# First scan step summed on TensorE, image 0's copy ahead of its shift: a four-layer residual stack on one core

## What is computed

```python
def _L0_conv_ref(x, w1, b1, w2, b2, w3, b3, alpha):     # layer 2 is the same
    xf = x.reshape(n, c, hw)
    e1 = jax.nn.relu(jnp.einsum('dc,ncp->ndp', w1, xf) + b1[None, :, None])
    e2 = jax.nn.relu(jnp.einsum('dc,ncp->ndp', w2, xf) + b2[None, :, None])
    assembly = jax.nn.relu(jnp.einsum('oc,ncp->nop', w3, xf) + b3[None, :, None])
    attn = jax.nn.softmax(jnp.einsum('ndi,ndj->nij', e1, e2), axis=-1)
    out = jnp.einsum('ncj,nij->nci', xf, attn)
    return (alpha[0] * out + assembly).reshape(n, c, h, w)

def step(prev, x_i):                                     # layer 1; layer 3 has relu for the slope
    y = jnp.einsum('oc,nch->noh', Wc, prev) + conv_b[None, :, None]
    y = jnp.where(y >= 0, y, prelu_a * y)
    cur = y + x_i
    return (cur, cur)

x = x + layer_l(_gn(x))                                  # for l = 0, 1, 2, 3
```

## Time and profile before

| | us |
|---|---|
| median of the three runs | 257.13 (256.96 to 257.18) |
| the profiled execution | 256.91 |
| its span, first to last instruction | 255.1 |
| TensorE busy (products / weight loads) | 245.5 / 218.1 |
| VectorE busy | 171.8 |
| ScalarE busy | 95.6 |
| GpSimd busy | 86.6 |

### The profile page before, as it was taken

One profiled execution on the slowest core, in us unless ns is written; L12 is line 12 of the kernel. 1 busy time (PEld: TensorE's weight loads), 2 busy tenths in 40 slices (PEclk: granted clock), 3 DMA queues, 4 the chain that ended last, 5 costly groups with the idle time before them and its releaser, 6 DMA issues.

```text
span 255.1 us, 11065 instructions
## 1 busy us (share of the span) xinstructions
PE 245.5 (96%) x4485; PEld 218.1 (85%) x4488; DVE 171.8 (67%) x667; ACT 95.6 (37%) x229; POOL 86.6 (34%) x135
## 2 busy tenths in 40 slices
PE   6997999999978999999999999999999999999995
PEld 2776888888668999999997787878786999999995
DVE  2779857475767777777789785666758555555453
ACT  2144463724963343434445445454557100000000
POOL 0206600004346656666732310000062433243332
PEclk9999999999999999999999999999999999999999
DMA  6999000000000000000000000000000000011212
GB/s 219 393 374 421 37 0 0 4 0 0 0 4 3 0 0 0 1 0 0 0 1 3 0 0 4 0 0 0 1 3 0 3 0 0 0 41 62 82 62 82
DMA packets 5199, 11.47 MB, mean 45 GB/s; under 512 B 704, under 2 KB 3264, under 8 KB 4672
## 3 DMA queue, kind: packets, MB, share of 16 engines
q1 hardware_dynamic: 4896, 10.76, 11.4%
q10 hardware_dynamic: 288, 0.52, 0.6%
HBM read 9.19 MB, written 2.10 MB: 44 GB/s over the span
## 4 chain that ended last, share of the span: by engine, by line
PE 88%; DVE 6%; DMA 2%; POOL 2%; issue 1%; ACT 0%; POOLq 0%; DVEq 0%; ACTq 0%
PE banks L494 43%; PE banks L391 20%; PE banks L456 11%; PE banks L403 6%; PE banks L422 2%; DMA x<-in_x 2%; PE banks L334 1%; PE banks L441 1%; PE banks L477 1%; DVE st L682 1%; POOL rstd L1065 1%; DVE mx L792 1%; PE banks L358 1%; DVE sloped L923 0%; PE banks L369 0%
## 5 line engine op out<-in xcount | busy, mean ns | idle before, releaser
L494 PE MATMUL banks<-state,wc 128*64 128x64 f32 x3840 | 114.9, 223 | 2.7 <-DVE state L933 1.3
L494 PEld LDWEIGHTS banks<-state,wc 128*64 128x64 f32 x3840 | 114.1, 138 | 3.7 <-DVE state L933 1.6
L391 PE MATMUL banks<-xn,w 128*128 128x256 f32 x256 | 61.0, 384 | 0.0
L391 PEld LDWEIGHTS banks<-xn,w 128*128 128x128 f32 x256 | 47.1, 190 | 7.2 <-issue 1.7
L1065 POOL TENSOR_TENSOR rstd<-gvar,mhalf 128x2 f32<-128x2 f32 (+1 forms) x12 | 15.2, 1279 | 104.2 <-DVE gvar L757 100.2
L906 DVE SCALAR_TENSOR_TENSOR state<-banks,negb,inb 128x64 f32<-128x64 f32 x116 | 29.1, 281 | 24.1 <-PE banks L494 24.0
L923 DVE SCALAR_TENSOR_TENSOR sloped<-banks,par,share 128x64 f32<-128x64 f32 x116 | 29.7, 281 | 14.1 <-PE banks L494 12.0
L456 PE MATMUL banks<-probT,xT 128*128 128x256 f32 x128 | 29.0, 380 | 1.4 <-DVE probT L830 1.4
L456 PEld LDWEIGHTS banks<-probT,xT 128*128 128x128 f32 x128 | 24.3, 190 | 5.0 <-issue 1.8
L631 ACT COPY banks<-inb 128x256 f32 (+1 forms) x29 | 10.9, 376 | 31.9 <-DVE state L933 29.4
L1122 POOL TENSOR_TENSOR share<-share,bent 128x256 f32<-128x256 f32 x29 | 17.7, 612 | 4.1 <-ACT share L632 3.2
(11 more groups left out here) (113 smaller groups left out, 228.5 us busy)
## 6 DMA issues: line engine op xcount, KB each, us to landing
w<-in_w SPq DMA_DIRECT2D x2, 1024.0 KB, 12.0
xT<-in_xT SPq DMA_DIRECT2D x4, 512.0 KB, 12.3
wc<-in_wc SPq DMA_DIRECT2D x2, 1024.0 KB, 17.5
result<-xh SPq DMA_DIRECT2D x15, 128.0 KB, 1.8
x<-in_x SPq DMA_DIRECT2D x3, 512.0 KB, 8.4
x<-in_x ACTq DMA_DIRECT2D x1, 256.0 KB, 4.3
x<-in_x SPq DMA_DIRECT2D x1, 256.0 KB, 4.1
w<-in_w ACTq DMA_DIRECT2D x1, 256.0 KB, 4.8
```

The costliest lines, as they stand in the source:

```text
L391: mm = nc.tensor.matmul(bank[2 + m // 2][:, m % 2 * POS:(m % 2 + 1) * POS], w3[l][:, k, m * P:(m + 1) * P], xn_s[:, k], start=(k == 0), st ...
L494: mm = nc.tensor.matmul(bank[K * h + m][c:c + TILE, 0:COLS], wc[l][:, k, m * P + c:m * P + c + TILE], state[:, h, k], start=first and not ...
```

## The change

- *Step 0 of the first scan.* `prelu_sum` and its semaphores go. The products of step 0 leave their accumulation open, and TensorE adds the inputs by products with the identity matrix (`add_inputs`): for output columns 0 and 1 after the last product of column 2, for columns 2 and 3 at the end. VectorE then makes slope and maximum from the bank.
- *Shares of steps 0 and 1 in parts.* ScalarE makes them for the first three images ahead of the last image's inputs, and for the last image when `early` is there; of the four late input columns (L616) one instead of two goes ahead of that.
- *GpSimd in the first scan.* The biased share of step 1 goes ahead of the keeping of state 0, and the sum for the very last step (L1118) behind the keeping of states 1 and 2. The loop starts at state 3 and keeps a state before it does the next share, where it did the share first; both orders are the same sequence.
- *Image 0 of layer 0.* The copy of half 1 of `probT` goes ahead of `shifted_input` and of all four residuals.
- *The power of layer 0* is taken for image 1 alone first (four columns) and then for images 2 and 3 (eight columns), each with its own negated mean and shift; the waits on `norm[0].done` and `s_shift` count one more.
- *Layer 2's signed weights* wait for outputs of layer 0: the small ones for the first of image 0, the large ones for the first of image 1 (two columns) and of image 2 (two columns).
- *Passage into layer 2.* The means stand behind three groups of transposes, not four, the variances behind five, not six; two of image 1's four statistics go behind the normalised image.

```diff
+        def power_rounds(l):
+            rounds = [(r, c0, c1) for r, (c0, c1) in enumerate(norm_rounds(l))]
+            return rounds if l else [rounds[0], (1, K, 2 * K), (1, 2 * K, NC)]
...
+            def add_inputs(ms):
+                s = scan[1]
+                for m in ms:
+                    if m == 0:
+                        pe.wait_ge(s.inb, NC - K)
+                        pe.wait_ge(s.early, K + 1)
+                    nc.tensor.matmul(bank[m][:, 0:COLS], ident[:], inb[:, 1, m], start=False, stop=True,
+                                     skip_group_check=True).then_inc(s.y[m], 1)
...
+                alone = l == 1 and not seeded
...
-                            state[:, h, k], start=first and not seeded, stop=final, skip_group_check=True)
-                    if final:
+                            state[:, h, k], start=first and not seeded, stop=final and not alone,
+                            skip_group_check=True)
+                    if final and alone:
+                        add_inputs({2: (0, 1), 3: (2, 3)}.get(m, ()))
+                    elif final:
                         mm.then_inc(s.y[m], 1)
...
-                    turn(range(0, 4))
+                    turn(range(0, 3))
                     group_means(l, r)
-                    turn(range(4, 6))
+                    turn(range(3, 5))
                     group_variances(l, r)
-                    turn(range(6, 8))
+                    turn(range(5, 8))
...
-                        act.wait_ge(norm[l].done, 2)
+                        act.wait_ge(norm[l].done, 2 if first or l else 3)
...
-                scan_inputs(1, 1, (N - 1,), EARLY, range(K // 2))
+                ready, late = slice(0, (N - 1) * T), slice((N - 1) * T, COLS)
+                def first_share(q, places):
+                    return nc.scalar.activation(share[:, q, :, places], inb[:, q + 1, :, places], ACT.Identity,
+                                                scale=oma[:, 0:1])
                 act.wait_ge(s.inb, NC - K)
+                first_share(0, ready)
+                first_share(1, ready)
+                scan_inputs(1, 1, (N - 1,), EARLY, range(1))
                 act.wait_ge(s.early, K + 1)
-                step_inputs(0, 1, 0)
-                step_inputs(1, 2, 1)
-                scan_inputs(1, 1, (N - 1,), EARLY, range(K // 2, K))
+                first_share(0, late).then_inc(s.share, 1)
+                act.wait_ge(s.cleared, 1)
+                nc.scalar.copy(banks[:, K:2 * K, 0:COLS], inb[:, 2]).then_inc(s.seeded, 1)
+                first_share(1, late).then_inc(s.share, 1)
+                scan_inputs(1, 1, (N - 1,), EARLY, range(1, K))
...
-                        shifted_input()
+                        if l == 2:
+                            shifted_input()
...
-                    add_residual(0)
-                    add_residual(1)
+                    late = first and l == 0
+                    early = 0 if late else 2
+                    for m in range(early):
+                        add_residual(m)
                     dve.wait_ge(s.pt_mm, n * PC + 2)
                     nc.vector.tensor_copy(by_rows(l, probT[:, 1]), in_order(l, bank[0][:, 0:POS])).then_inc(s.pt_copied, 1)
-                    for m in range(2, by_vector[l] if last else K):
+                    if late:
+                        shifted_input()
+                    for m in range(early, by_vector[l] if last else K):
                         add_residual(m)
...
-                        for k in range(K):
-                            prelu_sum(q, t, h, k)
...
-                    image_stats(l, 1)
+                    image_stats(l, 1, range(K // 2))
                 normalise_first(l)
+                if l == 2:
+                    image_stats(l, 1, range(K // 2, K))
...
-                for r, (c0, c1) in enumerate(norm_rounds(l)):
-                    width = K // 2 if c1 - c0 == K else c1 - c0
+                for r, c0, c1 in power_rounds(l):
+                    width = K // 2 if c1 - c0 == K and (l, r) != (0, 1) else c1 - c0
...
+                if l == 1:
+                    share_bias(1, 1)
+                    pool.wait_ge(s.sloped[K - 1], 1)
+                nc.gpsimd.tensor_tensor(inb[:, 0], state[:, 0], bias, ALU.add).then_inc(s.taken, 1)
+                def keep_state(t, h):
+                    for u in units:
+                        pool.wait_ge(s.state[u], t + 1)
+                    nc.gpsimd.tensor_tensor(inb[:, t], state[:, h], bias, ALU.add).then_inc(s.taken, 1)
+                    if l == 1:
+                        share_bias(t + 1, 1 - h)
+                keep_state(1, 1)
+                keep_state(2, 0)
+                pool.wait_ge(s.taken, 1)
+                nc.gpsimd.tensor_tensor(by_image(inb[:, 0]), by_image(inb[:, 0]), xr[:, 0], ALU.add).then_inc(s.last_in, 1)
+                with pool.Fori(0, (T - 4) // 2) as i:
                     for h in range(2):
+                        keep_state(i * 2 + 3 + h, 1 - h)
...
+                        pool.wait_ge(att[0].x_done, 1 if done is s_signed12 else K * (1 + k // 2) + 1)
                         nc.gpsimd.tensor_tensor(w[:, k], w[:, k], sign[:, 0:1].to_broadcast([P, w.shape[2]]), ALU.mult)\
                             .then_inc(done, 1)
```

More of the change, by code:

```diff
@@ L120, in __init__ @@
             self.sloped = [sem(f"sloped_branch_ready_{u}") for u in units]
-            self.summed = [sem(f"first_products_summed_{u}") for u in units]
             self.cleared = sem("banks_cleared")
@@ L624, in step_inputs @@
                 s = scan[1]
-                if isinstance(q, int) and q == 1:
-                    act.wait_ge(s.cleared, 1)
-                elif not (isinstance(q, int) and q == 0):
-                    for k in range(K):
-                        act.wait_ge(s.state[k], q)
-                if not (isinstance(q, int) and q == 0):
-                    nc.scalar.copy(banks[:, K * h:K * h + K, 0:COLS], inb[:, t]).then_inc(s.seeded, 1)
+                for k in range(K):
+                    act.wait_ge(s.state[k], q)
+                nc.scalar.copy(banks[:, K * h:K * h + K, 0:COLS], inb[:, t]).then_inc(s.seeded, 1)
                 nc.scalar.activation(share[:, h], inb[:, t], ACT.Identity, scale=oma[:, 0:1]).then_inc(s.share, 1)
@@ L682, in column_stats, with image_stats @@
                 nc.vector.bn_stats(st[:, n * K + k].rearrange("p a b -> p (a b)"), src).then_inc(norm[l].stats, 1)
-            def image_stats(l, n):
-                for k in range(K):
+            def image_stats(l, n, ks=range(K)):
+                for k in ks:
                     if l == 0:
@@ L777, in shifted_input @@
                     def shifted_input():
-                        dve.wait_ge(s_shift, (1 if first else 2) + l)
+                        dve.wait_ge(s_shift, (1 if first else 2 if l else 3) + (3 if l else 0))
                         for m in range(K):
@@ L908, in relu_state, with prelu_sloped @@
                         .then_inc(s.result if is_last(q) else s.state[k], 1)
-                def summed(q, k, h):
-                    return rest[:, k] if isinstance(q, int) and q == 0 else product(k, h)
-                def prelu_sum(q, t, h, k):
+                def prelu_sloped(q, t, h, k):
                     dve.wait_ge(s.y[k], q + 1)
-                    nc.vector.tensor_tensor(rest[:, k], product(k, h), inb[:, t, k], ALU.add).then_inc(s.summed[k], 1)
-                def prelu_sloped(q, t, h, k):
-                    if isinstance(q, int) and q == 0:
-                        dve.wait_ge(s.summed[k], 1)
-                    else:
-                        dve.wait_ge(s.y[k], q + 1)
-                    nc.vector.scalar_tensor_tensor(sloped[:, k], summed(q, k, h), par[:, PA_1:PA_1 + 1],
+                    nc.vector.scalar_tensor_tensor(sloped[:, k], product(k, h), par[:, PA_1:PA_1 + 1],
                                                    share[:, h, k], ALU.mult, ALU.add).then_inc(s.sloped[k], 1)
@@ L930, in prelu_state @@
                         nc.vector.scalar_tensor_tensor(new_state(q, h, k), sloped[:, k], bent[:, k:k + 1],
-                                                       summed(q, k, h), ALU.add, ALU.max).then_inc(s.state[k], 1)
+                                                       product(k, h), ALU.add, ALU.max).then_inc(s.state[k], 1)
                         return
                     nc.vector.tensor_tensor(new_state(q, h, k), like_new(q, sloped[:, k]),
-                                            like_new(q, summed(q, k, h)), ALU.max)\
+                                            like_new(q, product(k, h)), ALU.max)\
                         .then_inc(s.result if is_last(q) else s.state[k], 1)
@@ L1078, in inverse_std @@
                         pool.wait_ge(s_small, 32)
-                        pool.wait_ge(s.done, r + 1)
+                        pieces += 1
+                        pool.wait_ge(s.done, pieces)
```

(12 more changed lines are left out.)

9 lines of the change are left out of this document (1 added, 8 removed).

## The result

The changed kernel takes 253.8 us (253.75 to 254.28) beside 257.12 us (256.96 to 257.18) before: a ratio of 0.9876 [0.9859, 0.9893], 3.3 us less. Its profiled execution took 253.8 us with a span of 252.0. The forecast was 253.6, with 252.8 to 255.2 as range.

The account below looks back on a forecast made before the run. TensorE holds 88% of the chain of waits, so time comes only from its waits or a shorter list. Gains 1.64 + 1.60 + 0.25 = 3.5 off 256.91 give 253.4, as a median 253.6; range 252.8 to 255.2.

Parts of the forecast that it names:

- (a): Image 0 of the first attention: with the copy ahead of the shift, TensorE's wait before the output vanishes; gain 1.64.
- the split of the power: Layer 0's power for twelve columns cut in two, four columns first: costs and gains nothing by itself.
- the gain would shrink to nothing but 0.1: Layer 2's weight products left beside image 1's shifted image: VectorE at 30.0, scores ending at 28.37, (a) nearly lost.
- rival 2: Moved weight products hold VectorE in the output phases of images 1 and 2: 255.1 for half, 256.6 whole; chance 0.07.
- (b): First scan's steps 0 and 1: step 1 starts 0.17 earlier, step 2 at 75.65 instead of 77.25; gain 1.60.
- the 0.24 and the 0.1: Step 0 of the first scan: 0.24 us per identity product and 0.1 per switch of tiling mode.
- next to nothing: Step 0: cost of TensorE's new wait for the last inputs, ready at 72.01 when 13 of 16 pairs end at 72.0.
- State 0 was in time: First scan: state 0 of step 0 ready at 73.3, before step 1's start at 73.65.
- Rival 1: Each switch of tiles drains the array, 0.28 more three times; gain (b) 0.75, time 254.5; chance 0.14.
- GpSimd's tie in step 1: Step 1's first slope: GpSimd's L1115, done at 74.95, comes last by 0.1, after the product at 74.85.
- rival 4: GpSimd's new order leaves it late in all 28 scan steps: slower, 257.2 or 259.2; chance 0.05.
- (c): Passage from the first scan to the second attention: the 0.20 of idle and a little overlap; gain 0.25.

Follow-up runs that it names:

- a_copy_behind: The changed kernel with image 0's copy put back behind the shifted image and two residuals: 255.58 us.
- after: The changed kernel itself, with the whole change applied to the kernel before: 253.80 us.
- b_tiled_adds: The changed kernel with each identity product made as two 64-column tiles, so the tiling mode never switches in step 0: 253.92 us.
- b_tiled_fewer_waits: The changed kernel with identity products in 64-column tiles and VectorE's two waits for the inputs ahead of step 0 taken out: 253.91 us.
- b_sums_in_banks: The changed kernel without identity products; VectorE adds step 0's inputs and writes the sum back into the bank: 253.89 us.

## Why the forecast held, step by step

- **(a) 1.64 forecast, 1.63 measured** (1.56 at image 0's output, 0.07 in image 1), and a_copy_behind gives all of it to the copy. L460 ended at 24.05, not 23.86, because the load was 0.18 longer. That the split of the power is worth nothing held.
- **The weight products**: the move was right, its price was not. The step "the gain would shrink to nothing but 0.1" put the cost of leaving them at about 1.5; it is 0.48. It compared VectorE with the end of the scores, as if TensorE needed the softmax then. Sixteen branch products stand between. At their new place they hold nobody, so rival 2 didn't happen: from output to output images 2 and 3 last 13.36 and 14.17, as they did before (timeline of after):

```profile
36.63 1.04 POOL L1183 TENSOR_TENSOR w<-w,sign 128x512 f32<-128x512 f32 x1 [11.16 <-DVE xw L872]
36.86 0.47 DVE L872 SCALAR_TENSOR_TENSOR xw<-banks,rstd,rx 128x256 f32<-128x256 f32 x1
```

- **(b) 1.60 forecast, 1.43 measured.** The mis-sized term is step 0: 3.44 instead of 3.23 (1.94 + 0.96 + 0.3, and the rounding up to 73.65). By pieces: the first add started 1.76 after the step, where 13 pairs alone were put at 1.58. Each two identity products and a switch took 0.59, and three pairs and a switch 0.50; the forecast's own terms make 0.58 and 0.46. So the 0.24 and the 0.1 were good, and 0.18 of the miss lies ahead of the first add, in the wait for the last inputs that the forecast held to cost "next to nothing": they were ready when forecast (L917 ends at 70.55, 1.59 after the step), but 0.17 pass from there to the add. There are four switches before step 1 and the sum had three; that isn't the reason, for b_tiled_adds, without a switch, has its first add at 1.74. State 0 was in time only just: it was done at 72.17, 3.21 after the step and not 2.9, because VectorE's first slope came late (b_tiled_fewer_waits); the sum has no term for that, and it cost nothing only because TensorE was late too (b_tiled_adds). The 1.43 come from step 1: 1.47 there, and -0.04 in step 0, where the forecast had 1.43 and 0.17.
- **Rival 1** isn't borne out. A switch costs about 0.1: passes of the adds start 0.11 apart, and the first tile behind them 0.20 after the last. The page named there (the Trainium skill, TensorEngine Tiling (Array Packing), Tiling Modes, Key Properties) says that it drains TensorE, and a pass's whole 0.28 on top doesn't fit into 0.59 for four passes, which would take some 0.48 without a switch by the forecast's estimate (2 x 0.24).
- **GpSimd's tie in step 1** was near: L1144 was put last by 0.1 and ended at 73.48, 0.22 ahead of the slope. The slope came 1.30 after the step, as forecast, and 0.1 later than in the steps behind it; whether GpSimd or TensorE set that 0.1 isn't shown. GpSimd wasn't late for good either (rival 4): steps 2 and 3 start 1.93 apart, the length of a step in the earlier trace rows.
- **What the forecast had for the wrong reason**: it costed the identity products as the price of taking VectorE's sums away. The sums are free (b_sums_in_banks). What matters is that the sum stays in a bank, and that only since GpSimd's share now runs beside VectorE's slopes: a coupling between two edits that it costed apart. In the kernel before, slopes with two operands in SBUF took 0.28 each while GpSimd stood idle (its 3.19 in the earlier trace rows). With the sums in SBUF, 1.2 of the gain would have been lost.
- **(c) 0.25 forecast, 0.22 measured**: 0.14 as idle and overlap at L407, and 0.08 within the attention, of which no single wait in the trace gives account. The forecast had put all of it at L407, so the near match of the sum is in part luck.

## What to carry to other kernels

When work moves beside GpSimd, look where each VectorE instruction has its operands: with one of them in a bank it kept its 0.28 us, with both in SBUF it waited until GpSimd was done. Price a late step at the instruction that needs its result, after counting what the waiting engine still has in its list (0.48 instead of 1.5 here). And when two engines are level in a stage, shortening one of them only moves the wait: four cheaper products gave 0.09 and a new idle of 0.58.

## What was not expected of the hardware

- A short VectorE instruction (275 ns) that met GpSimd with two SBUF operands took 634 and 655 ns: until GpSimd's ended.
- In one execution 1.57 and 0.24 of idle TensorE, close together, were followed by about 3.4 us at 1.2 GHz; in all others of this study's profiles the scan ran at 2.4 GHz.
- VectorE let 0.95 us pass between its last input and its first slope in three kernels (after and the two tiled ones), with or without two waits in between. The cause wasn't found.
